# A graph layer on one core: GpSimd makes one-hots between its gathers, the third stage loads two of three of them, one-hots are 76 wide, sigmoids run in five batches

## The reference

```python
total_edge = jnp.concatenate([node_feats[src], node_feats[dst], edge_feats], axis=-1)
nbr_filter = jax.nn.sigmoid(_bn(total_edge @ W1.T + b1, g1, bt1))
nbr_core = jax.nn.softplus(_bn(nbr_filter, g2, bt2))
h = nbr_filter * nbr_core
agg = jax.ops.segment_sum(h, dst, num_segments=N_NODES)
new_node = _bn(agg, g3, bt3)
return node_feats + new_node          # then _layernorm(x + that)
```

## Time and profile before

| | us |
|---|---|
| median of 3 runs | 2716.24 |
| the runs | 2714.34, 2720.82, 2716.24 |
| the profiled execution, own time | 2712.68 |
| its span | 2710.9 |
| busy: GpSimd, VectorE | 1971.0, 1034.9 |
| busy: TensorE, ScalarE | 883.8, 551.2 |

### The profile page before, as it was taken

The page is one execution under the profiler, slowest core; times in us unless marked ns, Lnnn a source line. Parts: engine busy times, 40 slices in busy tenths (PEclk is TensorE's granted clock), DMA queues, the critical chain, the costliest instruction groups (busy, mean ns, idle before and its releaser), DMA issues. The chain is left out here.

```text
span 2710.9 us, 20494 instructions
## 1 busy us (share of the span) xinstructions
PE 883.8 (33%) x5714; PEld 444.2 (16%) x5714; DVE 1034.9 (38%) x1548; ACT 551.2 (20%) x530; POOL 1971.0 (73%) x1869
## 2 busy tenths in 40 slices
PE   4323222222222222222222213213213210277776
PEld 3101000000000000000000001001001000176762
DVE  2323223213213223221322223223212439899997
ACT  1000000000000000000000000000000039799974
POOL 7777777777777777777777777777777741287763
PEclk8655555556555555555555555555555555599998
DMA  7546445435435435443544335448554549898952
GB/s 204 141 109 160 120 101 140 112 82 139 111 83 140 111 92 130 111 104 90 140 111 113 102 90 144 99 116 253 150 136 113 143 141 384 313 308 293 298 150 96
DMA packets 247392, 404.68 MB, mean 149 GB/s; under 512 B 66782, under 2 KB 132124, under 8 KB 234736
## 3 DMA queue, kind: packets, MB, share of 16 engines
q1 hardware_dynamic: 141417, 290.49, 35.8%
q0 software_dynamic: 50048, 51.30, 10.5%
q10 hardware_dynamic: 55819, 61.63, 7.2%
HBM read 295.52 MB, written 107.76 MB: 149 GB/s over the span
## 5 line engine op out<-in xcount | busy, mean ns | idle before, releaser
L402 POOL DMA_INDIRECT rows<-p_table,src_idx x1496 | 1413.9, 945 | 473.7 <-issue 427.4
L580 ACT ACTIVATE z_sb<-z_ps 128x512 f32<-128x512 f32 x196 | 116.6, 596 | 1996.0 <-remote 975.7
L477 PE MATMUL z_ps<-into_z,with_w 128*64 128x512 f32 (+1 forms) x784 | 375.5, 1057 | 444.1 <-issue 323.2
L730 DVE TENSOR_TENSOR z_sb<-z_sb,xg_ps 128x512 f32<-128x512 f32 x141 | 96.6, 685 | 1061.6 <-remote 420.7
L453 PE MATMUL xg_ps<-ident,rows 128*128 128x128 f32 x564 | 155.8, 431 | 843.2 <-DMA rows<-p_table,src_idx 631.3
L453 PEld LDWEIGHTS xg_ps<-ident,rows 128*128 128x128 f32 x564 | 100.0, 215 | 1070.1 <-DMA rows<-p_table,src_idx 780.0
L702 DVE TENSOR_TENSOR into_z<-d_in,node_ps 84x1024 f32<-84x1024 f32 x196 | 235.2, 1201 | 101.6 <-DMA d_in<-dst_f 72.2
L1022 POOL TENSOR_TENSOR h_buf<-h_buf,s_all 128x1536 f32<-128x1536 f32 x66 | 223.5, 3440 | 59.3 <-ACT h_buf L993 59.3
L423 POOL MEMSET pace<- 128x1280 f32 x187 | 221.4, 1184 | 0.1
L732 DVE BATCH_NORM_STATS2 stats<-z_sb 128x512 f32 (+1 forms) x196 | 135.6, 692 | 72.2 <-DVEq L727 30.7
L730 DVE TENSOR_TENSOR z_sb<-z_sb,q_ps 128x512 f32<-128x512 f32 (+1 forms) x47 | 31.9, 678 | 339.3 <-remote 152.9
(11 more groups left out here) (151 smaller groups left out, 809.6 us busy)
## 6 DMA issues: line engine op xcount, KB each, us to landing
s_all<-edge_mem SPq DMA_DIRECT2D x102, 768.0 KB, 7.6
d_in<-dst_f SPq DMA_DIRECT2D x97, 672.0 KB
edge_mem<-z_sb ACTq DMA_DIRECT2D x97, 512.0 KB
into_z<-e_main SPq DMA_DIRECT2D x98, 336.0 KB
near<-near_mem SPq DMA_DIRECT2D x65, 504.0 KB, 4.9
near_mem<-near_one SPq DMA_DIRECT2D x97, 336.0 KB
rows<-p_table,src_idx POOLq DMA_INDIRECT x1496
agg<-edge_mem SPq DMA_DIRECT2D x8, 768.0 KB
```

The costliest lines, as they stand in the source:

```text
L402: gp.indirect_dma_start(out=to[0:size.tile, t, h, :], out_offset=None, in_=table, in_offset=bass.IndirectOffsetOnAxis(ap=which, axis=0)).t ...
L477: mm = pe.matmul(to[h * F:(h + 1) * F, 0:w], which(h)[0:height], into_z[s][0:height, h, 0:w], start=first, stop=last)
L580: act.activation(z_sb[s][:, 0:size.half], z_ps[s % 2][:, 0:size.half], ACT.Copy).then_inc(e_copied, 1)
L730: v.tensor_tensor(z, z, xg_ps[s][:, part], ALU.add).then_inc(z_copied, 1)
```

## The change

It has four parts.

- GpSimd no longer clears `pace` behind the gathers of groups 8 to 194. It makes one-hots of *second* halves there instead (`near_two_of`): four `tensor_scalar` of 128x76, one per tile of 128 edges, each comparing the row 0, 1, 2, ... with the edge's place, which is a pointer operand. Groups 8 to 15 make two groups' one-hots each, so that all 195 are covered. The wait for the last one stays. For the x groups the memset stays, but it clears `stats` (1176 columns), and VectorE waits for all eight before its first group.
- SP stores them to a new `near_two_mem`, pair by pair, ahead of the store to `near_mem`.
- In the third stage SP loads the second-half one-hots of the first two groups of a chunk in a further DMA; VectorE makes those of the third group alone. One-hots, sums and adds are 76 wide instead of 84.
- The chunks that get their sigmoid in the third stage are the same in number (38), but in five runs (8, 8, 8, 7, 7) instead of seven (6, 6, 6, 6, 6, 6, 2); a run takes in the rest.

```diff
-        near_mem = dram("near_mem", [GROUPS, P, TILES * WIN])
+        near_mem, near_two_mem = (dram(n, [GROUPS, P, TILES * Q_ROWS]) for n in ("near_mem", "near_two_mem"))
...
-        READY_RUNS, GATE_RUNS = (range(18, 24), range(36, 42), range(54, 58)), (
-            range(12, 18), range(24, 30), range(30, 36), range(42, 48), range(48, 54), range(58, 64), range(64, CHUNKS + 1))
+        READY_RUNS, GATE_RUNS = (range(20, 24), range(32, 36), range(44, 48), range(55, 59)), (
+            range(12, 20), range(24, 32), range(36, 44), range(48, 55), range(59, CHUNKS + 1))
...
+                def store_near_two(j, s):
+
+                    sp.wait_ge(near_two_made, j * 2 + 2)
+                    sp.dma_start(near_two_mem[bass.ds(j * 2, 2)].rearrange("k p w -> p k w"),
+                                 near_two[s][:].rearrange("p k t n -> p k (t n)")).then_inc(near_two_stored[s], 16)
...
                     spread_dst(j)
+                    if not isinstance(j, int) or j >= 1:
+                        store_near_two(j - 1, 1 - s)
                     if not isinstance(j, int) or j >= 2:
                         store_near(j - 2, s)
...
+                def near_two_of(n):
+
+
+                    j, k = n // 2, n % 2
+                    if k == 0 and j >= 2:
+                        gp.wait_ge(near_two_stored[j % 2], 16 * (j // 2))
+                    for t in range(TILES):
+                        ones = gp.tensor_scalar(near_two[j % 2][:, k, t], iota_row[:, 0:Q_ROWS], rel[:, n, TILES + t:TILES + t + 1], None, ALU.is_equal)
+                    ones.then_inc(near_two_made, 1)
+                    gp.wait_ge(near_two_made, n + 1)
+
                 for g in range(X_GROUPS):
                     gather(g, FULL, x)
-                    gp.memset(pace[:], 0.0).then_inc(paced, 1)
-                    gp.wait_ge(paced, g + 1)
+                    gp.memset(stats[:], 0.0).then_inc(cleared, 1)
+                    gp.wait_ge(cleared, g + 1)
                 gp.wait_ge(p_stored, 16 * BLOCKS)
+                gp.wait_ge(made, 3)
                 for g in range(X_GROUPS, GROUPS):
                     gather(g, FULL, p_table)
-                    gp.memset(pace[:], 0.0).then_inc(paced, 1)
-                    gp.wait_ge(paced, g + 1)
+                    if g == X_GROUPS:
+                        gp.wait_ge(places_made, 2)
+                    if g < 2 * X_GROUPS:
+                        near_two_of(2 * (g - X_GROUPS))
+                        near_two_of(2 * (g - X_GROUPS) + 1)
+                    else:
+                        near_two_of(g)
...
                 v.wait_ge(flag_set, 1)
+                v.wait_ge(cleared, X_GROUPS)
...
+            LOADED = CHUNK - 1
...
                         sp.dma_start(near_by_half[m.slot % 2][:, :, 0].rearrange("p k t n -> p k (t n)"),
                                      near_mem[bass.ds(m.c * CHUNK, CHUNK)].rearrange("k p w -> p k w")).then_inc(near_loaded[m.slot % 2], 16)
+                        sp.dma_start(near_by_half[m.slot % 2][:, 0:LOADED, 1].rearrange("p k t n -> p k (t n)"),
+                                     near_two_mem[bass.ds(m.c * CHUNK, LOADED)].rearrange("k p w -> p k w")).then_inc(near_loaded[m.slot % 2], 16)
...
-                                equal(near_by_half[m.slot % 2][:, :, 1], rel[:, m.c * CHUNK:(m.c + 1) * CHUNK, TILES:]).then_inc(near_ready, 1)
+                                equal(near_by_half[m.slot % 2][:, LOADED, 1], rel[:, m.c * CHUNK + LOADED, TILES:]).then_inc(near_ready, 1)
```

More of the change, by code:

```diff
@@ L191, in build @@
             d_in = sb("d_in", [WIN, 2, 2, HALF])
-            near_pair = [sb(f"near_one{s}", [P, 2, TILES, WIN]) for s in range(2)]
+            near_pair = [sb(f"near_one{s}", [P, 2, TILES, Q_ROWS]) for s in range(2)]
+            near_two = [sb(f"near_two{s}", [P, 2, TILES, Q_ROWS]) for s in range(2)]
             base_all = sb("base_all", [P, HALVES])
@@ L229, in build @@
             iota_p = sb("iota_p", [P, 1])
-            pace = sb("pace", [P, 1280])
-            paced = sem("paced")
+            cleared, near_two_made = sem("cleared1"), sem("near_two_made")
+            near_two_stored = [sem(f"near_two_stored{s}") for s in range(2)]
             win_col = sb("win_col", [P, WINDOWS])
@@ L373, in all_groups @@
                     sp.wait_ge(near_made, PAIRS_OF)
-                    sp.dma_start(near_mem[GROUPS - 1], near_pair[(PAIRS_OF - 1) % 2][:, 0].rearrange("p t n -> p (t n)")
-                                 ).then_inc(near_stored[(PAIRS_OF - 1) % 2], 16)
+                    last = (PAIRS_OF - 1) % 2
+                    sp.dma_start(near_mem[GROUPS - 1], near_pair[last][:, 0].rearrange("p t n -> p (t n)")).then_inc(near_stored[last], 16)
+                    sp.wait_ge(near_two_made, GROUPS)
+                    sp.dma_start(near_two_mem[GROUPS - 1], near_two[last][:, 0].rearrange("p t n -> p (t n)")).then_inc(near_two_stored[last], 16)
                     for s in range(2):
                         sp.wait_ge(near_stored[s], 16 * ((PAIRS_OF - s + 1) // 2))
+                        sp.wait_ge(near_two_stored[s], 16 * ((PAIRS_OF - s + 1) // 2))
                     sp.wait_ge(z_ahead, 16 * (EARLY + C_SLOTS))
@@ L909, in build @@
             near = [sb(f"near{s}", [P, CHUNK * 2 * TILES, WIN]) for s in range(2)]
-            near_by_half = [near[s][:].rearrange("p (k h t) n -> p k h t n", k=CHUNK, h=2) for s in range(2)]
+            near_flat = [near[s][:].rearrange("p j n -> p (j n)") for s in range(2)]
+            near_by_half = [near_flat[s][:, 0:CHUNK * 2 * TILES * Q_ROWS].rearrange("p (k h t n) -> p k h t n", k=CHUNK, h=2, n=Q_ROWS)
+                            for s in range(2)]
+            LOADED = CHUNK - 1
+            near_rest = [near_flat[s][0:T_P, 0:2 * T_TILES * Q_ROWS].rearrange("p (j n) -> p j n", n=Q_ROWS) for s in range(2)]
             near_w = near[0]
@@ L930, in build, with sum_of @@
                 sem(n) for n in ("h_turned", "rows_ready", "near_ready", "summed", "rel_made", "win_near", "win_summed", "win_added"))
[L932 to L933 removed]
+            def sum_of(k, h, wide):
+                return sum_ps[h * F:(h + 1) * F, k * WIN:k * WIN + wide]
             def here(m):
@@ L1026, in _, with window_sums @@
             def _(pe):
-                def window_sums(m, k, hots):
+                def window_sums(m, k, hots, wide):
                     n = m.size
@@ L1032, in window_sums @@
                         for h in range(2):
-                            mm = pe.matmul(sum_of(k, h), h_rows[m.slot % 2][0:n.tile, k, t, h * F:(h + 1) * F],
+                            mm = pe.matmul(sum_of(k, h, wide), h_rows[m.slot % 2][0:n.tile, k, t, h * F:(h + 1) * F],
                                            hots[0:n.tile, h * n.tiles + t, :], start=(t == 0), stop=(t == n.tiles - 1))
@@ L1048, in step @@
                             if m.size is FULL:
-                                pe.wait_ge(near_loaded[m.slot % 2], 16 * (m.turn * (S // 2) + m.slot // 2 + 1))
+                                pe.wait_ge(near_loaded[m.slot % 2], 32 * (m.turn * (S // 2) + m.slot // 2 + 1))
                         pe.wait_ge(rows_ready, m.c + 1)
@@ L1056, in step @@
                                     after(pe, win_added, m.c * CHUNK)
-                                window_sums(m, k, near[m.slot % 2][:, 2 * TILES * k:2 * TILES * (k + 1)]).then_inc(summed, 1)
+                                hots = (near_by_half[m.slot % 2][:, k].rearrange("p h t n -> p (h t) n") if m.size is FULL else
+                                        near_rest[m.slot % 2])
+                                window_sums(m, k, hots, Q_ROWS).then_inc(summed, 1)
                             else:
@@ L1073, in equal @@
                     n = len(shape) - 2
-                    row, at = iota_ps[0:shape[0], :], places
+                    row, at = iota_ps[0:shape[0], 0:shape[-1]], places
                     row = row.rearrange("p (a n) -> p a n", a=1) if n == 1 else row.rearrange("p (a b n) -> p a b n", a=1, b=1)
@@ L1083, in dst_of, with add @@
                     return table[:, bass.ds(m.c * CHUNK + k, 1), :].rearrange("p g j -> p (g j)")
-                def add(k, h, base):
-                    lanes = agg[h * F:(h + 1) * F, bass.ds(base, WIN)]
-                    return v.tensor_tensor(lanes, lanes, sum_of(k, h), ALU.add)
+                def add(k, h, base, wide):
+                    lanes = agg[h * F:(h + 1) * F, bass.ds(base, wide)]
+                    return v.tensor_tensor(lanes, lanes, sum_of(k, h, wide), ALU.add)
                 def copy_rows(m):
@@ L1152, in step_general @@
                                 v.wait_ge(win_summed, g * WINDOWS + w + 1)
-                                add(k, 0, w * WIN)
-                                add(k, 1, w * WIN).then_inc(win_added, 1)
+                                add(k, 0, w * WIN, WIN)
+                                add(k, 1, w * WIN, WIN).then_inc(win_added, 1)
                     if m := back(0):
```

18 lines of the change are left out of this document (8 added, 10 removed).

## The result

The changed kernel takes **2841.35 us** (median of 3 runs, 2838.56 to 2842.77) against 2716.24 before: a ratio of 1.0457, 95% interval 1.0443 to 1.0471. The forecast was 2665 in a range of 2612 to 2735, and faster. It is slower by 125 us, and outside the range. The profiled execution has a span of 2836.7 us, 125.8 more than before.

What follows compares the result with a forecast made beforehand. GpSimd was taken to bound the first stage, DMA the second, VectorE and ScalarE the third. Terms -221.4 + 175.5 - 0.7 + 5 - 9 = -51 us against 2716.2 gave 2665 us, range 2612 to 2735.

Steps and rivals of the forecast that it cites:

- Step 1: First stage, GpSimd: 187 memsets of 1.184 us go, 221.4 us less, all on the path.
- Step 2: First stage, GpSimd: 780 compares of 128x76 at 0.225 us add 175.5 us, a gain of 46 against the memsets.
- upper bound: First stage: price limit per compare from the 128x128 tensor_tensor, 0.455 us, giving 355 us for all compares.
- Step 3: x groups: shorter memsets save 0.7 us, but VectorE waits for the eighth, shifting z work 9 to 16 us; taken as +5.
- Step 4: SP's store of near_two_mem ahead of each pair's loads: z starts some 8 us behind the gathers instead of 3; cost 0.
- Steps 5 to 8: VectorE's first stage 0; third stage: VectorE 0.8 us less per chunk, ScalarE's end -10, transfers hidden, +1 for jams: -9.
- D: Third stage: us of transfer per chunk, estimated 4.04 to 4.88, taken as 4.2 and hidden; zero gain at 4.57.
- rival D: First stage: the one-hots pipeline like memsets at 0.16 us each, 125 us in all, ending at 2616; chance 0.10.
- rival C: Third stage becomes DMA-bound at 4.88 us a chunk: +16 instead of -9, ending at 2690; chance 0.10.
- A: First stage: one-hots cost more than the memset; at 0.40 us each +91 us, ending at 2802; chance 0.13.
- B: First stage: z chain needs no less than 11.14 us a group, so the gain becomes holds, leaving 2712; chance 0.12.

Runs made afterwards that it cites:

- e2: Changed kernel with each of a group's four compares cut to 8 of 76 columns; 2715.8 us (one run), a group's compares 1.14 us.
- e1: Changed kernel with one compare of 304 columns per group in place of four of 76; 2696.4 us (one run), beside a kernel before of 2692.8.
- e3: Changed kernel with an immediate 0.0 in place of the pointer to the compared number; 2773.5 us (one run), a group's compares 1.51 us.
- e12: e4 with all three second halves of a chunk loaded, none made by VectorE in the third stage; 2739.6 us, ratio 1.0032 to the kernel before.
- e19: e4's kernel unchanged, on a chip where the kernel before took 2730.7 us; 2714.0 us, ratio 0.9933.
- e20: e4 with a pause of two 200-column memsets behind each group's gathers, beside a kernel before of 2730.7 us; 2727.8 us, ratio 0.9989.
- e4: Changed kernel with VectorE making the second halves in stage one, GpSimd without compares or memset from group 8 on; 2462.44 us, ratio 0.9149 to the kernel before.
- e9: Kernel before without its memset and the wait behind it from group 8 on; 2477.16 us, ratio 0.9191 to the kernel before.
- e5: e4 without the eight memsets behind the x gathers and VectorE's wait for them; 2458.04 us, ratio 0.9122 to the kernel before.
- e10: e4 with the seven sigmoid runs of the kernel before in place of five; 2718.9 us, ratio 0.9957 to the kernel before.

## Why the prediction was wrong

**Step 1** was right: the memsets' 221.4 us went.

**Step 2 failed**, and alone makes the sign. "One input of SBUF and one output make it nearest to the affine_select of 128 columns, 0.293 us" chose the wrong neighbour. The compare took 0.458 us in place of 0.225, and 780 of them 357 us in place of 175.5. That this is the value of the upper bound (0.455) is luck: by the split measured in e2 a compare as wide as that row, 128 columns, would take 0.59 us (an estimate), so the "upper bound" was none. The 0.10 us fixed came from memsets, which read nothing, and the 1.5 ns a column from one affine_select less that 0.10; both were carried over to an operation that reads a tile and a pointer: 0.265 us and 2.54 ns (e1 to e3). The work of a group in four instructions paid the fixed part four times. The rule of the Trainium skill that stood beside the step (GPSIMD Engine Reference, Performance pitfalls for Q7 kernels) gives an estimate of 1.7 ns a column, from its 2.03 cycles an element at 1.2 GHz; measured are 2.54. The same page of the Trainium skill (Elementwise — side-by-side cycle accounting) has about 2.6 cycles an element for an operation with two inputs, an estimate of 2.2 ns at that clock, and the trace shows more than that even for one tile and a pointer.

**A second effect was not in the sum**: the first gather behind four compares takes 1.03 us in place of 0.95, +14 us over the stage.

**Step 3** took +5 and was 0. VectorE's first hots came at 98.40 us in place of 80.84, 17.6 later, a little more than the 9 to 16 worked out, but GpSimd was never held.

**Step 4** was right in its mechanism and its cost of 0. SP's waits for the one-hots and z's start behind the gathers, in the changed kernel's timeline and PE's waits:

```profile
923.53 0.49 SPq L357 DMA_DIRECT2D into_z<-e_main  x1
924.20 0.96 SPq L360 DMA_DIRECT2D with_w<-q_table  x2
...
930.78 1.97 PE L506 MATMUL z_ps<-into_z,with_w 128*64 128x512 f32 x4 [7.52 <-DMA into_z<-e_main]
```

```profile
PE z_ps L506 <- DMA into_z<-e_main: 568.2, 79, 11.1
```

z starts 10.1 us behind the last gather's end at 920.67 (8 were expected). What it waits for is `e_main`, which lands some 7 us after SP issued it, and not the q loads, which SP issued in 0.96 us here and not in 4.2. GpSimd, which sets the turn, is never held by it.

**Steps 5 to 8** held. VectorE's one-hots in the third stage, its wait for sums and PE's for the loads:

```profile
L1115 DVE TENSOR_TENSOR near<-iota_ps,rel 128x304 f32<-128x304 f32 x65 | 30.8, 474 | 2.8 <-DVE iota_ps L1198 0.8
```

```profile
DVE agg L1125 <- PE sum_ps L1069: 35.4, 51, 3.9
```

```profile
PE sum_ps L1069 <- DMA near<-near_two_mem: 41.7, 37, 2.8
```

0.474 us where 0.44 was worked out, 35.4 where "some 35" stood, 41.7 at the end of "10 to 40". ScalarE is 5.7 us shorter (279.0 to 273.3; 5.1 forecast), the last add comes 10.7 sooner (10, less 1 for jams). D, taken as 4.2 us, stayed hidden; at 359 GB/s 1.565 MB are 4.36, still under the 4.57 at which the gain would be zero by that step's formula. (By the same formula D = 4.48 gives -5 and not -6, and rival D's compares 2615 and not 2616; nothing rests on either.) e12, with 1.72 MB, passed it and lost 20 us: rival C's mechanism exists, one load further on.

**The rivals.** A happened: "a turn above 11.2 us proves A", and it is 11.92. It had 0.13, and its price of 0.40 us was still too low. The argument for it named the row of 0.455; the argument against was a likeness of operand counts. B, too, is real on a part of the chips. It was dismissed because "in all of the stage the holds add up to 22.8 us, so over its length the chain does follow". e19 and e20 show the fault in this: few holds at a turn of 11.14 say that the chain can do 11.14, not that it can do 10.9. On a chip like that of the first measurement, compares of 0.225 us would by e20 have given the first stage next to nothing. That last sentence is argued from another kernel's runs, not shown with such compares, and the changed kernel's own order on SP may matter, since it was not late there.

## What to carry to other kernels

A price that no row shows is bounded by its neighbours, and when the break-even (0.284 us) lies between the bounds (0.14 and 0.455), the choice of a neighbour is the forecast. A row of another operation is no bound at all until its own fixed part is known. Split a short operation into a part per instruction and a part per column with rows of its own kind, not of memsets, and count how many instructions pay the fixed part; here 304 columns in one instruction cost 1.06 us in place of 1.83 (e1, which compares all four tiles with the first tile's numbers; a form with the right numbers wasn't tried), and that only ties with the kernel before. VectorE, idle three quarters of the stage, does a pair's 608 columns in 0.78 us, which is where e4 puts them. Before work is put in the place of a pause, try what the pause is worth: e9, two lines shorter than the kernel before, is 8% faster on some chips. Where a chain has not been seen at a shorter turn, few holds at the present one don't show that it would follow.

The version that beats both kernels is e4 (or e5): a ratio of 0.915 to the kernel before on one kind of chip and 0.993 on the other, and by the medians 0.956 to the changed kernel on the second kind (2714.0 to 2839.7, measured beside a before of 2731 and 2730). Against the changed kernel on the first kind it wasn't measured.

## What was not expected of the hardware

GpSimd's fp32 compare of a 128-partition tile with a number per partition costs 0.265 us an instruction, 0.08 of it for the pointer, and 2.54 ns a column, as measured at 8, 76 and 304 columns.

One kernel has two speeds, by chip or by session: e4's took 2462 to 2463 on two occasions and 2714 on a third, each within 0.3% in its runs. On the slower kind ScalarE's copies start up to 40 us behind the recorded matmuls that they wait for, and up to 21.5 us behind everything that the profile shows them waiting for, in stretches of several groups. The transfers' packets don't tell the two apart (gathered rows of 2048 bytes took 171 ns on average in e4 and 174 in e10, between 300 and 1900 us). The cause is open. That the changed kernel, with 11.92 us a turn, shows none of it on the slower kind is measured twice; why, is not known.
